# Layer 0 of a four-layer image network: the stores of the depthwise results move from the sync engine's queue to the scalar engine's

## The reference, cut to what matters

```
x = x + L0(gn(x))   # the layer of this case
x = x + L1(gn(x))   # attention over channels
x = x + L2(gn(x))   # selective scan
x = x + L3(gn(x))   # depthwise 7x7 convolution

# L0
base = conv1x1(x, w_qkv)                       # 192 -> 576 channels
qkv  = concat([dwconv(base, w_dw3, 1),         # three depthwise convolutions,
               dwconv(base, w_dw5, 2),         # 3x3, 5x5 and 7x7,
               dwconv(base, w_dw7, 3)], axis=1)  # 3 * 576 channels
qkv  = conv1x1(qkv, w_pconv)                   # 1728 -> 576
q, k, v = split(qkv, 3)                        # attention over channels, 8 heads, three top-k softmaxes
return conv1x1(out, w_proj)
```

## Time and profile before

| what | value |
|---|---|
| median of 3 runs | 3204.47 us (3198.21 to 3208.03) |
| the profiled execution, time | 3192.12 us |
| the profiled execution, span | 3190.3 us |
| mean granted TensorE clock | 0.862 of full speed |
| PE busy | 2387.6 us, 75% |
| ACT busy | 978.0 us, 31% |
| DVE busy | 1220.4 us, 38% |
| moved by q1 (SP) | 305.94 MB in 162216 packets |
| moved by q10 (ACT) | 6.29 MB in 12672 packets |

### The profile page before, as it was taken

The page is one execution under the profiler, slowest core; times in us unless marked ns, Lnnn a source line. Parts: engine busy times, 40 slices in busy tenths (PEclk is TensorE's granted clock), DMA queues, the critical chain, the costliest instruction groups (busy, mean ns, idle before and its releaser), DMA issues. The chain is left out here.

```text
span 3190.3 us, 37429 instructions
## 1 busy us (share of the span) xinstructions
PE 2387.6 (75%) x15968; PEld 1379.6 (43%) x15968; DVE 1220.4 (38%) x1081; ACT 978.0 (31%) x1264; POOL 812.5 (25%) x321
## 2 busy tenths in 40 slices
PE   3877878739999999995697938678677877877022
PEld 1566666627777777772352112223132212321022
DVE  4333434310000000004402160799499728974722
ACT  2344444410000000002210011666367526650400
POOL 1433334300000000000000000578188607870310
PEclk9989989869999999997795565799899989998556
DMA  5899999962122112102000110000000000002389
GB/s 180 273 296 310 292 302 283 267 225 86 49 90 90 65 70 90 45 1 84 9 1 29 46 48 20 0 0 0 0 1 0 0 0 1 0 16 66 107 226 272
DMA packets 175035, 314.40 MB, mean 99 GB/s; under 512 B 7049, under 2 KB 130185, under 8 KB 166217
## 3 DMA queue, kind: packets, MB, share of 16 engines
q1 hardware_dynamic: 162216, 305.94, 31.4%
q10 hardware_dynamic: 12672, 6.29, 0.7%
HBM read 185.59 MB, written 125.04 MB: 97 GB/s over the span
## 5 line engine op out<-in xcount | busy, mean ns | idle before, releaser
L589 PE MATMUL ps<-mem 128*128 128x288 f16 x5376 | 677.0, 286 | 50.9 <-DMA mem<-depthwise_out 50.9
L589 PEld LDWEIGHTS ps<-mem 128*128 128x128 f16 x5376 | 519.3, 98 | 194.5 <-issue 66.5
L1350 POOL TENSOR_TENSOR mem<-mem 128x1024 f32<-128x1024 f32 x48 | 113.1, 2356 | 1632.9 <-ACT mem L1340 1632.9
L1353 POOL TENSOR_TENSOR mem<-mem 128x1024 f32<-128x1024 f32 x192 | 448.3, 2353 | 40.8 <-ACT mem L1324 40.5
L434 PE MATMUL ps<-mem 56*96 56x256 f16 x5184 | 325.7, 288 | 105.8 <-DVE mem L527 96.4
L1298 PE MATMUL ps<-mem 128*128 128x512 f32 x768 | 379.3, 617 | 16.1 <-POOL mem L1353 13.2
L434 PEld LDWEIGHTS ps<-mem 56*96 56x96 f16 x5184 | 312.0, 130 | 127.4 <-DVE mem L527 102.8
L1381 DVE TENSOR_TENSOR_SCAN mem<-mem,ps 128x1024 f32<-128x1024 f32 x144 | 337.9, 2347 | 60.7 <-ACT mem L1331 37.2
L804 DVE MEMSET mem<- 96x96 f32 x2 | 0.3, 138 | 860.9 <-DMA mem<-in_tri 860.9
L527 DVE TENSOR_TENSOR mem<-ps,mem 96x1024 f16<-96x1024 f32 x144 | 171.3, 1217 | 274.6 <-ACT mem L472 274.6
L503 POOL TENSOR_TENSOR mem<-mem 120x2304 f16<-120x2304 f32 x36 | 163.7, 4548 | 342.0 <-ACT mem L465 342.0
(11 more groups left out here) (179 smaller groups left out, 2392.2 us busy)
## 6 DMA issues: line engine op xcount, KB each, us to landing
depthwise_out<-mem SPq DMA_DIRECT2D x36, 1536.0 KB, 15.6
mem<-depthwise_out SPq DMA_DIRECT2D x16, 3328.0 KB, 10.9
mem<-in_wd SPq DMA_DIRECT2D x40, 1080.0 KB, 17.4
mem<-base_phases SPq DMA_DIRECT2D x72, 504.0 KB
base_phases<-mem SPq DMA_DIRECT2D x56, 576.0 KB, 10.5
mem<-l_planes SPq DMA_DIRECT2D x48, 252.0 KB
mem<-in_x SPq DMA_DIRECT2D x4, 2048.0 KB, 10.9
l_planes<-mem SPq DMA_DIRECT2D x2, 4032.0 KB, 13.3
```

The source lines that it names most:

```text
L589: ins = nc.tensor.matmul(ps[:, 2 * (i % 2) + h, 0:HALF], d, pw[0:rows, wa, k, HALF * h:HALF * h + HALF], start=(k == 0 and n == 0), stop=( ...
L1353: nc.gpsimd.tensor_tensor(hh[:, n % 4, :], hh[:, n % 4, :], cs[:, n % 2, :], ALU.mult).then_inc(hc_pool, 1)
```

## The change

`store_out` leaves SP's stream. ACT now begins the same 36 stores, the one of batch n - 1 right after the cast of unit (n, 0), after waiting that DVE has ended batch n - 1, and the last one after the last unit. The semaphores counted are the same, SP still waits for all stores at the end of the stage, and all other transfers are begun by SP in the same order.

```
-            def store_out(n):
-                sp.wait_ge(dw_lo, UPB * (n + 1))
-                sp.dma_start(d_dram[6 * BP * n:6 * BP * (n + 1)].rearrange("(c k) f n -> (k f) c n", k=3), stg[n % 2][0:MD]
-                             ).then_inc(d_stored[n % 2], 16)
...
-                if n >= 1:
-                    store_out(n - 1)
-            store_out(NBATCH - 1)
...
+            def store_out(n):
+                act.wait_ge(dw_lo, UPB * (n + 1))
+                act.dma_start(d_dram[6 * BP * n:6 * BP * (n + 1)].rearrange("(c k) f n -> (k f) c n", k=3), stg[n % 2][0:MD]
+                              ).then_inc(d_stored[n % 2], 16)
...
                 for k in range(UPB):
                     unit(n, k)
+                    if k == 0 and n:
+                        store_out(n - 1)
+            store_out(NBATCH - 1)
```

## The result

The changed kernel takes 3243.8 us (median of 4 runs, 3239.2 to 3249.8) against 3206.3 for the kernel before: 1.0114 times as long, with an interval of 1.0074 to 1.0154. It is slower by some 37 us, where 20 were forecast, inside the range of 3183 to 3250. The profiled execution has a span of 3246.2 us.

The account below looks back on a forecast made before the run. The prediction took the full DMA engines to bound the stage: +21.6 us for 18 batches without base steps, 0 for 16 with them, -1.7 for the tail, about +20 on 3204.47, so 3224 us; range 3183 to 3250.

Parts of the forecast that it names:

- T = 14.05 us, +1.2 a batch: Layer 0 depthwise stage: a batch without base steps takes T, 14.05 us instead of 12.85, over 18 batches +21.6 us.
- rival (c): Much slower: ACT's issues block casts, or 9 KB taps rows go before 1 KB store packets; 3260 to 3275 us, chance 0.10.
- Nothing in the batches with base steps: In 16 longer batches the chain of stores is mostly covered: 0, bounds -1 and +2 us each.
- The price of mixture, -5.5%: Packets of two queues served together take 5.5% less engine time, as in layer 3: 0.7 us a batch.
- The last batches: Tail of the stage, from the landing at 630.66 to the last landing: 22.8 us instead of 24.5, so -1.7 us.
- ACT's issue: Each of the 36 store issues added on ACT takes 0.5 us, hidden by PE's own unit.
- Rival (a): Faster: DMA engines stay full and mixing two queues pays; 3177 us, or 3190 for half of it; chance 0.22.
- Rival (b): No change: backlog on SP's queue covers the gap and mixture brings nothing; 3204 us (3195 to 3214), chance 0.21.

Follow-up runs that it names:

- small taps: Taps laid out in 1 KB runs instead of 9 KB rows: 0.9991 in the changed kernel, 1.0038 with stores on SP, 0.9942 with the issue before unit 0.
- half stores: Kernel with the issue before unit 0, each store cut into two 768 KB halves with own landing waits, first half issued after unit 2 of its batch: 3161.5 us, 0.9868.

## Why the prediction was right or wrong

The direction and the mechanism were right: the DMA engines bound the stage, the store's issue is chained to the landing of the one before, and in the gap the engines run dry. ACT's wait went from 133 to 187 us, and the DMA share in the batches without base steps from 0.99 to 0.92 (0.9 was forecast). The experiment without the chain takes most of the loss away, and that with a later issue makes it grow. Of the other signs, the stores didn't land as much sooner as I had said (median 14.5 us against 15.6; about 12 was forecast), and the longest got longer, 25.5 against 18.5.

The size came out at nearly double, and the sum was right in few of its terms. To see which, take the start of the cast of unit (n, 0), the same mark in both kernels, for n = 11, 12, 15 and 19: the turn out of the batches with base steps (11 to 12), the three turns without them (12 to 15) and four with them (15 to 19). The issues of the stores don't serve as such a mark: in the kernel before, the one at 288.34 stands 3.5 us behind the cast (11, 0), and the one at 341.10 3.8 us ahead of the cast (15, 0). Before:

```profile
284.84 2.83 ACT L472 CAST mem<-ps 96x1024 f16<-96x1024 f32 x3 [4.50 <-DMA depthwise_out<-mem]
...
304.99 2.83 ACT L472 CAST mem<-ps 96x1024 f16<-96x1024 f32 x3 [12.61 <-DMA depthwise_out<-mem]
...
344.90 2.83 ACT L472 CAST mem<-ps 96x1024 f16<-96x1024 f32 x3 [4.09 <-DMA depthwise_out<-mem]
...
412.71 2.83 ACT L472 CAST mem<-ps 96x1024 f16<-96x1024 f32 x3 [4.50 <-DMA depthwise_out<-mem]
```

and after:

```profile
305.27 1.01 ACT L464 CAST mem<-ps 96x1024 f16<-96x1024 f32 x1 [5.21 <-DMA depthwise_out<-mem]
...
330.90 1.01 ACT L464 CAST mem<-ps 96x1024 f16<-96x1024 f32 x1 [18.08 <-DMA depthwise_out<-mem]
...
373.18 1.01 ACT L464 CAST mem<-ps 96x1024 f16<-96x1024 f32 x1 [8.79 <-DMA depthwise_out<-mem]
...
448.82 1.01 ACT L464 CAST mem<-ps 96x1024 f16<-96x1024 f32 x1 [5.15 <-DMA depthwise_out<-mem]
```

Over the whole stage:

| turns of the cast (n, 0) | before, us each | after, us each | difference in all | forecast |
|---|---|---|---|---|
| 12 without base steps, inside a group | 13.1 | 14.1 | +11 | +14 |
| 4 out of the batches with base steps | 18.3 | 24.9 | +27 | +5 |
| 12 with base steps | 16.6 | 18.2 | +20 | 0 |
| the last four, to the end of the stage | | | -9 | +1 |
| the start, to the cast of unit (3, 0) | | | +1 | 0 |

The total is 50 us, for one pair of profiles. The run with one store in flight on SP, as fast as the kernel before, has 14.0, 17.5 and 16.7 us in the first three lines, so the second and the third are where the changed kernel loses. The terms are these:

- **T = 14.05 us, +1.2 a batch.** The mean inside a group is 14.1, but this is in part luck: I worked out an even turn, with each batch's own loads beside its store, and there is none. The turns from 448.82 on are 25.3 (the one out of the batches with base steps), 9.3, 10.8 and 25.3 us. In a long one the loads of more than two batches and base parts pass one store, 5.6 MB of q1 from 448 to 474, and then there is nothing left for the gap. The turn out of the batches with base steps, which I had counted at +1.2 like the others, costs +6.6. The taps' turns of 9 KB against 1 KB, which I had put into rival (c) with 0.10, belong in the forecast: with 1 KB runs the whole loss disappears.
- **Nothing in the batches with base steps.** They cost +1.7 each, near the upper bound of +2 that I had given. They are longer than the chain, as I had said, but their DMA share fell from 0.99 to 0.86.
- **The price of mixture, -5.5%.** It was +1.7% in this kernel against the profile before and +0.6% against the run with one store in flight on SP, so the 0.7 us a batch didn't come. It does come in the others with two queues: 520 against 539 us with the issue before unit 0 (-3.4%), 540 against 572 with small taps (-5.5%), 509 against 548 with half stores (-7.2%). Queues that run empty can't be all of the reason: with 1 KB taps the chained kernel has it too, 548 against 572 (-4.2%). The rule that I had set beside it, from the Trainium skill (DMA: Bandwidth & Descriptors, "Issuing engines are not separate DMA queues"), that spreading saves only issue time, isn't borne out here. With 1 KB taps, where the DMA engines are nearly full on either queue (5 and 9 us empty), the move to ACT, issued before unit 0, saves 32 us of engine time, and the ratio goes from 1.0038 to 0.9942.
- **The last batches.** From the landing that frees batch 34's unit 0 to the next stage it was 25.1 us before (630.66 to 655.75) and is 23.1 now (682.72 to 705.78): -2.0, with -1.7 forecast. But the three turns just before it, from cast (31, 0) to (34, 0), were quicker by 7 us, where I had counted +2.4. Why is open; it hides a part of the loss of the others.
- **ACT's issue.** 0.31 us each, 0.5 taken; no cast suffers visibly. The cast of 1.0 us ahead of the issue doesn't delay it at all (below), so the 1.05 us in each turn of the chain of stores was nothing. Without it my sum would have come out lower still.

Rival (a) was wrong as the outcome of this change, but it names what the better order gives: its 3177 to 3190 is where the kernels with an earlier issue are (3181.8 and 3189.3). Rival (b) fell. Of rival (c), ACT's issues didn't block, but the other half, the rows of 9 KB that take turns before the store, was a part of what happened.

A third staging tile, which would undo the chain without moving the issue, wasn't tried.

## What to carry to other kernels

When an engine's queue shares the DMA engines with another engine's, keep the wait for a transfer's landing behind the issue of the next transfer; here the order of two lines was worth 1.6%. On one queue the same chain cost nothing (1.0001). On a second queue the store is passed by what is begun meanwhile, about one packet for one, so large rows on the one queue starve small runs on the other. Give the second queue its work early, and in transfers whose landings can be waited for in parts. Look at the DMA share first: with full DMA engines a second queue gains only by what it takes off the price of the packets, and loses what it lets run empty. And measure a turn between the same mark in both kernels, not between two issues whose place in the batch changes.

## What the runs showed of the hardware

- A DMA issue on ACT doesn't wait for the end of the cast ahead of it: 448.84 against the cast from 448.82 to 449.83. I had counted 1.05 us. Where that cast itself has to wait for ACT to be free, the issue even starts 0.6 us before it (the cast of unit (21, 0) is the first of the two at 483.42):

```profile
481.41 2.11 ACT L457 CAST mem<-mem 120x2304 f16<-120x2304 f32 x1
...
482.79 0.31 ACTq L468 DMA_DIRECT2D depthwise_out<-mem  x1
483.42 2.02 ACT L464 CAST mem<-ps 96x1024 f16<-96x1024 f32 x2
```

- ACT's issue of 1.5 MB takes 0.31 us (0.369 at most), while the same issue on SP behind a full queue took up to 3.5. With half stores ACT's took up to 5.2.
- Two queues take turns packet by packet: 537 packets of q1 to 530 of q10 in 4 us beside windows of 1.1 KB runs, and 68 to 74 in 3 us beside rows of 9 KB. Beside taps and base parts together it was 174 to 270.
- With the stores on ACT and not chained to a landing, the same packets took 2.2 to 7.2% less engine time than on one queue (527 against 539, 509 against 548); what got cheaper was the window packets, 79 to 60 ns, while the store's went from 48 to 52.
